# Eight-layer gated stack: two layers as single runs, inputs laid out per partition, contexts padded to 128 rows

## The reference, cut to what matters

```python
x = x + tanh(g_xattn[i]) * attention_i(layernorm(x), ctx_1024, mask_i, ...)
x = x + tanh(g_ffn[i])   * ffn_i(layernorm(x), ...)
```

```python
x_int = clip(round(x / scale), -127, 127)                  # scale = max(act_scale, 1e-5)
x_dq  = nan_to_num(x_int * scale, nan=0.0, posinf=1e4, neginf=-1e4)
out   = x_dq @ (ternary_weight - 1).T + bias

logits = tokens @ router_w.T + router_b; probs = softmax(logits)
top_p, top_i = top_k(probs, 2); w = top_p / (sum(top_p) + 1e-10)
out = sum over the two of w * (tokens @ expert_weights[top_i])   # 8 experts
```

## Time and profile before

| Stretch, us | Work | PE | DVE | POOL | clock | DMA share | GB/s |
|---|---|---|---|---|---|---|---|
| 0 to 24 | opening block | 8.6 | 2.1 | 1.8 | 1.00 | 0.67 | 177 |
| 24 to 226 | first attention | 180.3 | 87.7 | 83.2 | 0.98 | 0.62 | 190 |
| 226 to 841 | mixture of experts | 442.5 | 168.0 | 128.9 | | | |
| 841 to 1026 | masked attention, block 1 | 119.7 | 92.2 | 96.9 | 0.87 | 0.53 | 163 |
| 1026 to 2282 | searched network | 1198.7 | 914.6 | 162.6 | 0.97 | 0.03 | 10 |
| 2282 to 3009 | many-headed attention | 691.6 | 455.3 | 120.6 | 0.97 | 0.08 | 22 |
| 3009 to 3133 | ternary layer | 51.4 | 102.6 | 39.2 | 0.70 | 0.01 | 3 |
| 3133 to 3323 | masked attention, block 3 | 123.9 | 119.3 | 116.7 | 0.85 | 0.52 | 160 |
| 3323 to 3645 | routed layer | 266.1 | 174.8 | 6.6 | 0.86 | 0.06 | 19 |

### The profile page before, as it was taken

The page is one execution under the profiler, slowest core; times in us unless marked ns, Lnnn a source line. Parts: engine busy times, 40 slices in busy tenths (PEclk is TensorE's granted clock), DMA queues, the critical chain, the costliest instruction groups (busy, mean ns, idle before and its releaser), DMA issues. The chain is left out here.

```text
span 3644.9 us, 63304 instructions
## 1 busy us (share of the span) xinstructions
PE 3082.7 (85%) x24124; PEld 2448.5 (67%) x24124; DVE 2116.5 (58%) x4699; ACT 1382.0 (38%) x2696; POOL 756.5 (21%) x1012
## 2 busy tenths in 40 slices
PE   6976799915768999999999997799999993574979
PEld 5864466503557999999999996477666762353767
DVE  3435111225526778787778775466666657674555
ACT  2421111102214555555555554466666660121000
POOL 2534100056500013012002102211111103472000
PEclk9987899956988999999999998799999996796979
DMA  7661111125540000000000000100000000262000
GB/s 199 200 227 46 54 46 47 46 69 143 178 151 1 2 1 2 2 2 1 1 2 2 2 1 1 50 18 19 23 19 18 19 10 5 84 191 81 16 8 18
DMA packets 123183, 182.56 MB, mean 50 GB/s; under 512 B 13501, under 2 KB 97412, under 8 KB 122670
## 3 DMA queue, kind: packets, MB, share of 16 engines
q1 hardware_dynamic: 100352, 123.44, 11.6%
q10 hardware_dynamic: 16398, 40.68, 3.2%
q0 software_dynamic: 6144, 14.50, 1.3%
HBM read 150.98 MB, written 27.79 MB: 49 GB/s over the span
## 5 line engine op out<-in xcount | busy, mean ns | idle before, releaser
L2084 DVE CUSTOM_DVE_ANT_0 probs<-ps,add 112x375 f32<-112x375 f32 x512 | 250.2, 546 | 59.0 <-PE ps L2212 55.4
L2140 ACT ACTIVATE probs<-probs,neg_top 112x375 f32<-112x375 f32 x512 | 281.8, 599 | 5.2 <-DVE neg_top L2084 3.8
L2687 PE MATMUL ps<-we,xn_t 128*112 128x256 f32 x1024 | 231.5, 390 | 15.9 <-DVE x_sb L2656 15.9
L1635 DVE TENSOR_REDUCE top<-ps 112x16 f32<-112x1792 f32 x96 | 194.4, 2025 | 60.0 <-PE ps L1851 58.4
L2687 PEld LDWEIGHTS ps<-we,xn_t 128*112 128x112 f32 x1024 | 187.2, 183 | 59.5 <-DVE x_sb L2656 16.7
L2237 PE MATMUL ps<-ident,probs 112*125 112x112 f32 x1536 | 222.5, 281 | 3.0 <-DVE probs_t L2091 3.0
L1236 DVE TENSOR_TENSOR hidden<-gated,ps 128x512 f32<-128x512 f32 x64 | 44.0, 688 | 302.7 <-PE ps L1279 302.7
L2091 DVE COPY probs_t<-ps 125x336 f32<-125x336 f32 x256 | 128.9, 504 | 151.4 <-PE ps L2237 151.4
L2237 PEld LDWEIGHTS ps<-ident,probs 112*125 112x125 f32 x1536 | 189.7, 188 | 30.9 <-issue 22.9
L1651 DVE TENSOR_TENSOR probs<-probs,inv_sum 112x1792 f32<-112x1792 f32 x96 | 194.4, 2025 | 3.3
L1639 DVE TENSOR_TENSOR probs<-ps,top 112x1792 f32<-112x1792 f32 x96 | 194.4, 2024 | 3.3
(11 more groups left out here) (378 smaller groups left out, 6430.6 us busy)
## 6 DMA issues: line engine op xcount, KB each, us to landing
ctx_t<-in_ctx_T_dram SPq DMA_DIRECT2D x128, 375.0 KB, 11.7
ctx_sb<-in_ctx_dram ACTq DMA_DIRECT2D x104, 375.0 KB
queue<-zeros SPq DMA_DIRECT2D x32, 256.0 KB, 6.4
rows<-queue SPq DMA_DIRECT2D x16, 512.0 KB, 4.6
outputs<-out SPq DMA_DIRECT2D x16, 512.0 KB, 2.9
mask_in<-in_mask_BxSxS_fk_dram SPq DMA_DIRECT2D x32, 164.1 KB
mask_in<-in_mask_BxSxS_ik_dram SPq DMA_DIRECT2D x32, 164.1 KB
we<-in_L_ffn_We_dram SPq DMA_DIRECT2D x18, 256.0 KB, 6.8
```

What stands on the lines that cost most here:

```text
L1635: dve.tensor_reduce(top[:, :, :], scores, AX.X, ALU.max).then_inc(s["top_done"], 1)
L2084: dve.tensor_tensor_reduce(out=probs[:, u, h, :], in0=k.ps[0:S, SCORE + h, 0:L], in1=add[:, j % 2, :], scale=1.0, scalar=BIG, op0=ALU.add, ...
L2140: act.activation(probs[:, u, h, :], probs[:, u, h, :], ACT.Exp, bias=neg_top[:, u, h:h + 1], scale=-1.0).then_inc(s["probs_done"], 1)
L2687: mm = pe.matmul(k.ps[0:S, Y + n % YB, 0:D], xn_t[:, j, c, :], we[:, e, c, :], start=c == 0, stop=c == DC - 1)
```

## The change

It has five parts.

1. The host lays the inputs out so that each partition's data of a transfer lies together (`_arranged`): weight chunks, bias columns, `x`, the two masks (two batches side by side in rows of 768 words) and `ctx_t` (both chunks, in rows of 768 words). The transfers' access patterns lose their rearrangement.
2. `ctx_sb` has 128 partitions; the host pads each context from 125 to 128 rows, and the matmuls read the first 125.
3. Masks come for two batches in one transfer, with three buffers of two; SP's order in the masked attentions is mask pair, `ctx_t`, `ctx_t`, with no load of a later batch ahead of batches 1 to 3. The experts' queue is read and written with four consecutive rows per partition.
4. The ternary layer is one block without a loop. ACT norms and divides by the scale in one operation, and its copy after the transpose multiplies by the scale; DVE clips and rounds two batches at once, compares and guards the transposed pair, and adds the residual of a pair; PE adds the bias with a matmul of one row of ones. Statistics of pair t + 6 stand in DVE's step t; POOL computes shifts and gains for the groups of pairs 0-1, 2-5, 6-10 and 11-15, and ACT waits for a group's `shifts_done`.
5. The routed layer is one block without a loop after its weights' block. SP doesn't wait for the experts, PE does before its first product. Two experts go in one matmul of 512 columns into one of five banks. The second 16 batches' statistics, norms, logits and weights are placed among the first half's experts. Comparisons with the expert index are done for 16 batches at once, in three operations for 32.

The diff, cut to its core:

```diff
-                    sp.dma_start(w.ctx_t[:, j % CT, :, :], k.ctx_t_dram[j].rearrange("(c p) l -> p c l", p=P)).then_inc(...)
+                    sp.dma_start(w.ctx_t[:, j % CT, :, :], k.ctx_t_dram[j]).then_inc(...)
-        k.ctx_sb = sb(nc, "ctx_sb", [KR, NB, KC, D], F32)
+        k.ctx_sb = sb(nc, "ctx_sb", [P, NB, KC, D], F32)
-act.dma_start(k.ctx_sb[:, j % NB, :, :], k.inputs["ctx_1024"][j % B].rearrange("(r c) d -> r c d", c=KC))
+act.dma_start(k.ctx_sb[:, j % NB, :, :], k.inputs["ctx_1024"][j % B])
...
+def _arranged(_np, name, a):
+    if name in _BY_CHUNK:
+        a = a.reshape(a.shape[:-2] + (-1, P, a.shape[-1])).swapaxes(-3, -2)
+    elif name in _COLUMNS:
+        a = a.reshape(a.shape[:-1] + (-1, P)).swapaxes(-2, -1)
+    elif name in _MASKS:
+        a = a.reshape(B // 2, 2, S, L).transpose(0, 2, 1, 3).reshape(B // 2, S, 2 * L)
+        a = _np.pad(a, ((0, 0), (0, 0), (0, ROW - 2 * L)))
+    elif name == "ctx_1024":
+        a = _np.pad(a.reshape(B, KR, KC, D), ((0, 0), (0, P - KR), (0, 0), (0, 0)))
+    elif name == "x":
+        a = a.transpose(1, 0, 2)
+    return _np.ascontiguousarray(a)
...
@@ masked_attention
+                for j in range(B):
+                    if j % 2 == 0:
+                        load_masks(j // 2)      # waits for masks_done 2 * (j // 2 - 2)
+                    load_ctx_t(j)               # waits for scores_done j - 3
...
@@ run_experts
-...k.queue[u * UR:(u + 1) * UR, :].rearrange("(t p) d -> p t d", p=P)
+...k.queue[u * UR:(u + 1) * UR, :].rearrange("(p t) d -> p t d", p=P)
...
@@ ternary_layer: ACT, DVE's steady step, PE
+                def normalise(p):
+                    act.wait_ge(s["shifts_done"], [p < p1 for _, p1 in GROUPS].index(True) + 1)
+                    if p >= 4:
+                        act.wait_ge(s["clipped"], p - 3)
+                    for u in range(2):
+                        j = 2 * p + u
+                        ins = act.activation(normal[:, p % 4, u, :], k.x_sb[:, j, :], ACT.Identity, bias=shift[:, j:j + 1], scale=gain[:, j:j + 1])
+                    ins.then_inc(s["normed"], 1)
+                def copy(p):
+                    if p >= 3:
+                        act.wait_ge(s["out_done"], p - 2)
+                    act.wait_ge(s["transposed"], p + 1)
+                    act.activation(steps_t[:, p % 3, :], k.ps[:, XT + p % 2, 0:2 * DC * S], ACT.Copy, scale=scale[:, :]).then_inc(s["copied"], 1)
+                pipeline(PAIRS, [(normalise, 0), (copy, 2)])
...
+                for t in range(PAIRS + 2):
+                    if t < PAIRS:
+                        clip(t)
+                    if 0 <= t - 1 < PAIRS:
+                        mark_nan(t - 1)
+                    if t < PAIRS:
+                        to_whole(t)
+                    if 0 <= t - 1 < PAIRS:
+                        guard(t - 1)
+                    if t + AHEAD < PAIRS:
+                        statistics(t + AHEAD)
+                    if t >= 2:
+                        residual(t - 2)
+                    if t + AHEAD < PAIRS:
+                        means(t + AHEAD)
...
+                    pe.matmul(k.ps[0:S, OUT + p % OUTS, :], k.ones[0:1, 0:S], bias[:, :], start=True, stop=False)
+                pipeline(PAIRS, [(transpose, 0), (add_bias, 1), (multiply, 1)])
...
@@ routed_layer: DVE after the first half's weights, PE
+                for j in range(0, BODY, 2):
+                    add_experts(j)
+                    if j < 4:
+                        ...                      # bn_stats and bn_aggr of 8 batches of the second half
+                    elif j < 8:
+                        ...                      # norm of 8 batches
+                    elif j == 8:
+                        shift_logits(1)
+                    elif j == 10:
+                        normalise(1)
+                        for i in range(BODY, B):
+                            find_best(i)
+                    elif j == 12:
+                        find_places(1)
+                        pick(1)
+                    elif j == 14:
+                        scale(1)
...
+                pe.wait_ge(experts_loaded, 16 * E3)
+                for j in range(0, BODY, 2):
+                    experts(j)
+                    if 4 <= j < 8:
+                        for i in range(BODY + 4 * (j - 4), BODY + 4 * (j - 4) + 8):
+                            transpose(i)
+                            if i > BODY:
+                                route(i - 1)
+                    elif j == 8:
+                        route(B - 1)
```

More of the change, by code:

```diff
@@ new lines, in ternary_layer @@
+        names = ("weights_loaded rows_loaded shifted scale_cut inverted weights_transposed weights_copied stats_done mean_done eps_added "
+                 "rstd_done scales_done shifts_done normed clipped rounded transposed copied masked guarded out_done residual_done")
+        s = {n: sem(nc, n) for n in names.split()}
+        ternary_i = sb(nc, "ternary_i", [P, DC, D], I32)
+        ternary = sb(nc, "ternary", [P, DC, D], F32)
+        w_t = sb(nc, "w_t", [P, DC, D], F32)
+        bias = sb(nc, "bias", [1, 2 * D], F32)
@@ new lines, in ternary_layer @@
+        scale = sb(nc, "scale", [P, 1], F32)
+        inv_scale = sb(nc, "inv_scale", [P, 1], F32)
+        stats = sb(nc, "stats", [S, B, 6], F32)
+        mean_var = sb(nc, "mean_var", [S, B, 2], F32)
+        var_eps = sb(nc, "var_eps", [S, B], F32)
+        rstd = sb(nc, "rstd", [S, B], F32)
+        gain = sb(nc, "gain", [S, B], F32)
+        product = sb(nc, "product", [S, B], F32)
+        shift = sb(nc, "shift", [S, B], F32)
+        normal = sb(nc, "normal", [S, 4, 2, D], F32)
+        whole = sb(nc, "whole", [S, 2, 2, D], F32)
@@ L2457, in residual @@
-                    def residual(j0):
-                        for j in range(j0, j0 + 4):
-                            x = batch(k.x_sb, first + j)
-                            dve.wait_ge(s["out_done"], j + 1)
-                            dve.wait_ge(s["bias_added"], j + 1)
-                            dve.scalar_tensor_tensor(x, k.ps[0:S, 2 + j % OUTS, 0:D], k.tg[0:S, 6:7], x, ALU.mult, ALU.add).then_inc(s["residual_done"], 1)
-                    pipeline(BODY // 4, [(lambda g: quantize(4 * g), 0), (lambda g: residual(4 * g), 1)])
@@ new lines, in _ @@
+                for p in range(2):
+                    statistics(p)
+                for p in range(2):
+                    means(p)
+                dve.wait_ge(s["rows_loaded"], 48)
+                dve.tensor_scalar(scale[:, :], scale[:, :], 1e-5, None, ALU.max).then_inc(s["scale_cut"], 1)
+                dve.wait_ge(s["scale_cut"], 1)
+                dve.reciprocal(inv_scale[:, :], scale[:, :]).then_inc(s["inverted"], 1)
+                for p in range(2, AHEAD):
+                    statistics(p)
@@ L2489, in product @@
                         for c in range(DC):
[L2490 to L2493 removed]
+                            at = (u * DC + c) * S
+                            mm = pe.matmul(k.ps[0:S, OUT + p % OUTS, u * D:(u + 1) * D], steps_t[:, p % 3, at:at + S], w_t[:, c, :], start=False, stop=u == 1 and c == DC - 1)
@@ L2624, in _, with normalise, find_best @@
-                    for j in range(BODY):
+                def normalise(g):
+                    cut = slice(g * BODY, (g + 1) * BODY)
+                    dve.wait_ge(s["exps_done"], g + 1)
+                    link(dve.tensor_reduce(total[:, cut], exps[:, cut, :], AX.X, ALU.add))
+                    link(dve.reciprocal(total[:, cut], total[:, cut]))
+                    link(dve.tensor_tensor(probs[:, cut, :], exps[:, cut, :], each(total[:, cut]), ALU.mult))
+                def find_best(j):
+                    dve.max(best[:, j, :], probs[:, j, :]).then_inc(s["best_found"], 1)
```

616 lines of the change are left out of this document (319 added, 297 removed).

## The result

The changed kernel takes 3456.4 us (median of 4 runs, 3453.0 to 3458.5) against 3641.4 us for the kernel before (also the median of 4 runs, three of them those above): ratio 0.9487, 95% interval 0.9475 to 0.9499, 185 us faster. The forecast was 3421 with a range of 3390 to 3470, from a sum of 222 against the profiled execution. The profiled execution took 3453.0 us with a span of 3451.2 us, so against the profiled execution of before the gain is 193.7 us of span.

| From ... to ...

What follows compares the result with a forecast made beforehand. Most of the span is full TensorE, left alone; losses lie in context DMA, masked-layer starts, stage ends, ternary and routed layers. 60 + 50 + 16 + 3 + 43 + 50 = 222 off 3646.9, less 3.7, gives 3421 us, range 3390 to 3470.

Steps and rivals of the forecast that it cites:

- Five engines: Context loads to 125 partitions use 5 of 16 DMA engines, at 120 GB/s; padding to 128 moves them to all 16.
- the pitch of 3.27, the start and the end of masked layer 1: Masked layer 1: 34.5 us from 3.27 us a batch, 12.7 at the start, 12.5 at the end; sum 60.
- First attention: Shorter issue of six context loads, the opening block and the stage end gain 16 us, range 4 to 20.
- Masked layer 3: Start and middle gain 39 us, end 11; sum 50, range 20 to 58; VectorE, not DMA, is late next.
- Ternary layer: Rewritten without a loop, it takes 81 us against 124: 43 gained, range 15 to 55.
- The three waits: Ternary layer: ACT's normalise of pairs 2, 6 and 11 waits for POOL; 4.3 us twice, 1.3 once, 10 in all.
- The steady pitch: Ternary layer: VectorE sets 3.5 us a pair with waits (3.0 to 5.3); TensorE needs 3.0 at full clock.
- Routed layer: Gains of 4.5 us before the statistics, 11 at the weights chain, 34.7 in the second half; sum 50, range 35 to 56.
- the narrow matmuls: Routed layer, second half: 16 transposes and routes stay on TensorE, at full clock 0.65 us each plus 1.5: 12 us.
- Weights and rows in longer pieces: Weights in 2 kB pieces, experts' queue rows in 4 kB, mostly hidden behind full engines: 3 us, range 0 to 8.
- Rival B: The ternary layer stays on a half-clock TensorE; 27 of its 43 us lost, 3448 us; chance 0.10.
- Rival C: Slower than before: row pitch or a padded partition puts the three transfers on few engines; chance 0.02.

Runs made afterwards that it cites:

- f1: The kernel before with only the natural context padded to 128 partitions; 3559.5 us, ratio 0.9763.
- f2: The changed kernel with the natural context loaded for 125 partitions only; 3539.4 us, ratio 0.9713.
- g1: The changed kernel with `keep` of masked layer 3 made by ACT instead of GpSimd; 3436.5 us, ratio 0.9422.
- g3: The changed kernel with the ternary layer's statistics in six smaller groups instead of four; 3442.0 us, ratio 0.9433.
- g4: The changed kernel without the ternary layer's bias matmul, its bias left out of the result; 3445.4 us, ratio 0.9445.
- h2: The changed kernel with the routed layer's second half transposed and routed in eight blocks of two batches instead of two of eight; 3441.8 us, ratio 0.9442.
- f3: The changed kernel with `ctx_t` in two pieces of 1,500 B per partition instead of one of 3,000 B; 3450.3 us, ratio 0.9465.
- g2: The changed kernel with masked layer 3's `keep` and the square of the row sum on ACT instead of GpSimd; 3438.1 us, ratio 0.9425.
- h1: The changed kernel with smaller ternary groups and the ternary bias added by GpSimd instead of a matmul; 3445.9 us, ratio 0.9443.
- f4: The changed kernel with one expert per matmul (256 columns) in the routed layer; 3462.9 us, ratio 0.9496.

## Why the prediction was right, and where its sum was not

- *Five engines, right.* f1 and f2 show it from both sides, 84 and 83 us. The gains from the pitch of 3.27, the start and the end of masked layer 1 came out at 34.8, 16.0 and 14.6 us for 34.5, 12.7 and 12.5.
- *First attention, right*: 16.6 for 16. The six loads' issue fell from 11.84 to 3.35 us in f1, which has only the pad; f1 shows 13.8 of the 16.6.
- *Masked layer 3, the step that failed.* "What is late next is VectorE, not DMA": it was GpSimd. The 39 us for start and middle were 27, the 11 of the end 9. The reading rested on 25.16 of 26 us for VectorE; the same row has GpSimd at 23.06, so near that it had to be priced too. In the kernel before, between 3200 and 3290 us, DMA-bound, GpSimd was the busiest engine, 68.84 of 90 us (VectorE 64.78). With GpSimd relieved (g1), batch 0 to 31 takes 110.8 us, close to the 113.6 that the sum had.
- *Ternary layer.* The three waits were named, but priced too low: the two long ones cost 5.4 us each for 4.3 (whose own terms add up to 4.55), and 1.7 us each in the next pair, since TensorE came back at half clock; together 14, which g3 takes away whole. That is 4 of the 7 us missing; the other 3 were not taken apart. The steady pitch was nearly right (3.33 us for 3.5), its owner not: it was TensorE (g3, g4), priced at 3.0, with VectorE close behind.
- *Routed layer.* 4.3 of 4.5 at its front. Behind it 34 for 46: the narrow matmuls were priced at full clock (12 us), but in their long blocks the clock fell, for them and for the experts behind (16.3 us and some 5 more). h2 gives back 11.3. The trace of before had a row against the price: from 3344 to 3361 us the same kind of block, 16 batches long, has TensorE busy for 16.93 of 17 us at clock 0.50.
- *Weights and rows in longer pieces*: f3 shows for `ctx_t` that shorter pieces change no time; for the weights and the queue's rows, priced at 3 us, no run shows the term.
- *The network's -4.5 us* need be no effect of the change: with the same stage code the variants of the changed kernel lie between 1258.3 us (g2) and 1262.8 (g3). The mixture differs likewise: from its first expert on 604.7 us here and 609.9 before, and 603.9 to 612.5 over the profiles of the changed kernel's variants. So the 5.3 of the table may be no more than that. What sets either was not tried.
- The three missed sums (14, 12 and 7 us) and the network, less some 9 us that came in elsewhere, make the difference between 222 and 194; the rest, to 185, is that the profiled run of before lies 5.5 us above its median and that of after 3.4 below its own. Some luck is in the total: those 9 us, more than half of them in masked layer 1, covered a quarter of what the three stages and the network missed.

Rival B (a half-clock ternary layer) held in stretches only: the clock over 2936 to 3011 us is 0.84. Rival C did not occur.

## What to carry to other kernels

When a bound is taken away, price every engine's work per step, with operations in the background included, and not only the one that is full in a short stretch: here three engines stood at 23 to 25 of 26 us. A wait in the middle of a pipeline costs what is queued behind it and then the restart at the lower clock (5.4 and 1.7 us here). Read a group's mean beside its shortest and longest instance: in h1 a mean of 619 ns was made of 0.42 and 1.48 us. And try the partition count of a load's destination first: three rows of padding were nearly half of this gain.

## What was not expected of the hardware

- The granted clock fell inside a block of some 45 narrow matmuls (8 batches; 0.66 over the stretch), some 1.9 us after a wait of 1.68 us and in f4 some 4.4 us after one of 0.90; in a block of 16 batches it stayed at 0.50 for 17 us with TensorE busy for 16.59 of them. Blocks of two batches between experts, without the wait, leave it at 1.00 (h2).
- Adds on GpSimd hold VectorE up one instruction at a time: in h1 most roundings keep their 0.42 us and three take 1.48. GpSimd's own `gain` takes up to 1.45 us for 0.3 there. Whether the longer `gain` of masked layer 3 (857 ns on average in the changed kernel, 588 in g1) has this cause was not tested.
- On GpSimd 112x375 elements cost 525 ns in a multiply and add, but 1582 to 1808 ns in a comparison of int32 with a multiply.
